# Softmax totals of the second attention with queries on partitions, and heads mixed apart and scaled while they are added

## The reference, cut to what matters

```
q, k, v = projections of the normalised x, per head
scores  = q k^T / sqrt(64), causal
pattern = softmax(scores)
z       = pattern v                       # per head, 64 wide
attn    = sum over heads of z W_O + b_O   # 128 wide
x       = x + attn * g
```

## Time and profile before

| | |
|---|---|
| median of 3 runs | 1403.93 us (1403.16 to 1404.53) |
| the profiled execution | 1399.64 us, span 1397.6 us |
| TensorE busy | 1311.2 us, 94% |
| VectorE busy | 1010.6 us, 72% |
| ScalarE, GpSimd busy | 751.9 us, 684.6 us |
| mean granted TensorE clock | 0.984 |

### The profile page before, as it was taken

One profiled execution on the slowest core, in us unless ns is written; L12 is line 12 of the kernel. 1 busy time (PEld: TensorE's weight loads), 2 busy tenths in 40 slices (PEclk: granted clock), 3 DMA queues, 4 the chain that ended last, 5 costly groups with the idle time before them and its releaser, 6 DMA issues.

```text
span 1397.6 us, 25505 instructions
## 1 busy us (share of the span) xinstructions
PE 1311.2 (94%) x9904; PEld 673.7 (48%) x9904; DVE 1010.6 (72%) x1499; ACT 751.9 (54%) x1208; POOL 684.6 (49%) x525
## 2 busy tenths in 40 slices
PE   5889999999999987989999999999999999999897
PEld 3763222222222256555555555555555555555554
DVE  7667888888888865766766766766766766766768
ACT  5476777877777873334444444344344444444343
POOL 4101150100001010568678777677677777777771
PEclk9899999999999998999999999999999999999999
DMA  1522410000000000000000000000000000000000
GB/s 36 178 100 80 125 27 1 1 1 1 1 1 1 2 1 1 1 1 1 1 1 1 1 1 1 1 1 0 1 1 1 1 1 1 1 1 1 1 16 16
DMA packets 18165, 21.50 MB, mean 15 GB/s; under 512 B 7784, under 2 KB 15872, under 8 KB 16512
## 3 DMA queue, kind: packets, MB, share of 16 engines
q1 hardware_dynamic: 18048, 19.88, 4.4%
HBM read 14.63 MB, written 5.24 MB: 14 GB/s over the span
## 4 chain that ended last, share of the span: by engine, by line
PE 43%; DVE 11%; ACT 3%; issue 1%; POOL 1%; DVEq 0%; POOLq 0%; ACTq 0%
PE psum L1839 13%; PE psum L1817 12%; DVE part_max L1981 4%; PE psum L1760 4%; DVE inv L2002 4%; PE psum L1820 3%; ACT prob L1924 3%; PE psum L1798 2%; PE psum L1747 2%; PE psum L1786 2%; PE psum L1738 1%; DVE z L2005 1%; PE psum L1740 1%; PE psum L1739 1%; PE psum L1765 1%
## 5 line engine op out<-in xcount | busy, mean ns | idle before, releaser
L1727 POOL TENSOR_TENSOR acc<-acc,prob 128x1024 f32<-128x1024 f32 (+3 forms) x250 | 493.6, 1974 | 87.9 <-ACT prob L1924 57.2
L1924 ACT ACTIVATE prob<-psum 128x1024 f32<-128x1024 f32 (+1 forms) x320 | 283.4, 897 | 350.1 <-PE psum L1820 343.6
L1981 DVE TENSOR_REDUCE part_max<-psum 128x2 f32<-128x1024 f32 (+2 forms) x320 | 337.0, 1064 | 167.9 <-PE psum L1760 83.2
L679 DVE TENSOR_SCALAR w<-psum 128x512 f32<-128x512 f32 x472 | 304.8, 687 | 59.3 <-PE psum L536 44.8
L630 ACT ACTIVATE w<-psum 128x512 f32<-128x512 f32 x552 | 293.8, 601 | 86.0 <-PE psum L536 85.7
L556 PE MATMUL psum<-w,v_cols 128*32 128x512 f32 x2048 | 274.1, 608 | 0.0
L1839 PE MATMUL psum<-prob,v_pair 128*64 128x512 f32 (+3 forms) x1280 | 250.2, 532 | 0.7 <-POOL prob L1695 0.7
L1817 PE MATMUL psum<-q_hi,k_hi 64*128 64x512 f32 (+3 forms) x640 | 138.6, 429 | 30.1 <-DVE part_max L1981 20.4
L1839 PEld LDWEIGHTS psum<-prob,v_pair 128*64 128x64 f32 x1280 | 87.4, 137 | 145.3 <-issue 134.3
L1760 PE MATMUL psum<-k_hi,q_hi 64*128 64x512 f32 (+3 forms) x640 | 132.2, 410 | 5.4 <-DVE part_max L1981 3.8
L1817 PE MATMUL psum<-q_lo,k_hi 64*128 64x512 f32 (+3 forms) x640 | 118.6, 366 | 0.0
(11 more groups left out here) (304 smaller groups left out, 1400.2 us busy)
## 6 DMA issues: line engine op xcount, KB each, us to landing
q_rows<-q_dram SPq DMA_DIRECT2D x12, 256.0 KB
k_rows<-k_dram SPq DMA_DIRECT2D x3, 1024.0 KB
x<-in_L_attn_x SPq DMA_DIRECT2D x4, 256.0 KB, 4.0
mask<-in_L_ffn_attention_mask SPq DMA_DIRECT2D x1, 1024.0 KB, 6.9
q_dram<-x_high SPq DMA_DIRECT2D x1, 1024.0 KB, 6.7
q_dram<-x_low SPq DMA_DIRECT2D x1, 1024.0 KB, 6.0
k_dram<-q_rows SPq DMA_DIRECT2D x1, 1024.0 KB, 8.1
k_dram<-k_rows SPq DMA_DIRECT2D x1, 1024.0 KB, 6.2
```

The costliest lines, as they stand in the source:

```text
L679: nc.vector.tensor_scalar(w[:, s % WR, 2 * m + 1, :], pair_bank[n % RING][1], 0.0, None, ALU.max)\
L1727: nc.gpsimd.tensor_tensor(sums, sums, prob[:, s % PR, :, q0:C], ALU.add).then_inc(summed, 1)
L1924: nc.scalar.activation(prob[:, s % PR, :, q0:C], unit_both[n % RING][:, :, q0:C], ACT.Exp, scale=SCALE)\
L1981: nc.vector.tensor_reduce(part_max[:, :, i, c], unit_both[n % RING][:, :, 0:cols], AX_X, ALU.max)\
```

## The change

The total turns round: acc is now the weight operand, 128 queries at a time, and one column of ones moves, so that side_bank gets the sums with queries on partitions, eight columns (four tiles, two heads). VectorE takes the reciprocal of 128x8 values. z is not scaled any more. The mix multiplies each head's 64 rows apart, into the two banks of its unit, and the addition to attn becomes eight fused operations that multiply a 128x128 block by its query's reciprocal and add it to attn. A mix stays one unit for a chunk; only the last chunk is mixed and finished in two units of two tiles, on the same path as the others.

```diff
-        LAST = [("mix", NP - 1, NC - 1)]
         HALVES = 2
+        LAST = [("mix", NP - 1, (NC - 1, half)) for half in range(HALVES)]
...
+        def tiles_of(g, half):
+
+            return range(half * TH, (half + 1) * TH) if g == FINAL else range(TC)
...
-        inv = sb("inv", [P, C])
+        inv = sb("inv", [P, 2, 2 * TC])
...
-                for m in range(2):
-                    last = nc.tensor.matmul(side_bank[HALF[m], :], sh.ones[:, 0:W], acc[:, g % 2, m, :],
-                                            start=True, stop=True)
+                for j in range(TC):
+                    for m in range(2):
+                        last = nc.tensor.matmul(side_bank[:, 2 * j + m:2 * j + m + 1], acc[:, g % 2, m, j * P:(j + 1) * P],
+                                                sh.ones[:, 0:1], start=True, stop=True)
                 last.then_inc(totalled, 1)
...
-            def mix(hp, qc):
-                to = room_for(("mix", hp, qc))
+            def mix(hp, qc, half):
+                to = room_for(("mix", hp, (qc, half)))
                 g = hp * NC + qc
-                if g != FINAL:
-                    pe.wait_ge(scaled, g + 1)
-                for j in range(TC):
-                    if g == FINAL and j % TH == 0:
-                        pe.wait_ge(final_scaled, j // TH + 1)
-                    last = nc.tensor.matmul(to[:, j // TH if g == FINAL else 0, j * P:(j + 1) * P],
-                                            z[:, g % 2, j * P:(j + 1) * P], wo[:, hp, :], start=True, stop=True)
-                    if g == FINAL and j % TH == TH - 1:
-                        last.then_inc(final_mixed, 1)
-                if g != FINAL:
-                    last.then_inc(unit_filled, 1)
+                pe.wait_ge(z_copied, g + 1)
+                for j in tiles_of(g, half):
+                    for m in range(2):
+                        last = nc.tensor.matmul(to[:, m, j * P:(j + 1) * P], z[HALF[m], g % 2, j * P:(j + 1) * P],
+                                                wo[HALF[m], hp, :], start=True, stop=True)
+                last.then_inc(unit_filled, 1)
...
-            def scale(g):
+            def invert(g):
                 dve.wait_ge(totalled, g + 1)
-                nc.vector.reciprocal(inv[:, :], side_bank).then_inc(inv_done, 1)
-                dve.wait_ge(inv_done, g + 1)
-                dve.wait_ge(z_copied, g + 1)
-                nc.vector.tensor_tensor(z[:, g % 2, :], z[:, g % 2, :], inv[:, :], ALU.mult).then_inc(scaled, 1)
+                nc.vector.reciprocal(inv[:, g % 2, :], side_bank[:, 0:2 * TC]).then_inc(inv_done, 1)
...
-            def add_mixed(hp, qc):
-                n = AT["mix", hp, qc]
-                tiles = slice(qc * TC, (qc + 1) * TC)
+            def add_mixed(hp, qc, half):
+                unit = ("mix", hp, (qc, half))
+                n = AT[unit]
+                g = hp * NC + qc
                 dve.wait_ge(unit_filled, n + 1)
-                nc.vector.tensor_tensor(attn[:, tiles, :], unit_both[n % RING][:, 0, :].rearrange("p (t d) -> p t d", d=D),
-                                        attn[:, tiles, :], ALU.add).then_inc(unit_freed[n % RING], 1)
-                if hp == NP - 1:
-
-                    wait_freed(dve, ("mix", hp, qc))
-                    finish(qc)
+                dve.wait_ge(inv_done, g + 1)
+                for m in range(2):
+                    for j in tiles_of(g, half):
+                        tile = attn[:, qc * TC + j, :]
+                        last = nc.vector.scalar_tensor_tensor(out=tile, in0=unit_both[n % RING][:, m, j * P:(j + 1) * P],
+                                                              scalar=inv[:, g % 2, 2 * j + m:2 * j + m + 1], in1=tile,
+                                                              op0=ALU.mult, op1=ALU.add)
+                    if m == 0:
+                        link(last)
+                last.then_inc(unit_freed[n % RING], 1)
...
-                if k == GROUPS - 1:
-                    base_final()
...
-            scale_final(0)
-            scale_final(1)
-            finish_final(0)
-            finish_final(1)
+            invert(FINAL)
+            for unit in LAST:
+                take(unit)
```

More of the change, by code:

```diff
@@ L1557, in attention1 @@
                     [("value", 0, 2)],
-                    [("project", 0, 3), ("turn", 0, 2), ("mix", 0, 0)],
+                    [("project", 0, 3), ("turn", 0, 2), ("mix", 0, (0, 0))],
                     [("value", 0, 3), ("project", 1, 0)]]
         WHOLE = [[("value", 0, 2)],
-                 [("value", 0, 3), ("mix", -1, 3)],
-                 [("mix", 0, 0), ("turn", 0, 2)],
+                 [("value", 0, 3), ("mix", -1, (3, 0))],
+                 [("mix", 0, (0, 0)), ("turn", 0, 2)],
                  [("project", 1, 0)],
                  [("project", 1, 1)],
-                 [("turn", 0, 3), ("mix", 0, 1)],
+                 [("turn", 0, 3), ("mix", 0, (1, 0))],
                  [("project", 1, 2), ("value", 1, 0)],
-                 [("mix", 0, 2), ("turn", 1, 0)],
+                 [("mix", 0, (2, 0)), ("turn", 1, 0)],
                  [("value", 1, 1)],
@@ L1633, in attention1 @@
         final_summed = sem("final_summed")
-        final_scaled = sem("final_scaled")
-        final_mixed = sem("final_mixed")
         z_copied = sem("z_copied")
@@ L1638, in attention1 @@
         inv_done = sem("inv_done1")
-        scaled = sem("scaled")
         result_step = sem("result_step")
@@ L1855, in fill @@
                 else:
-                    mix(hp, what)
+                    mix(hp, what[0], what[1])
             pe.wait_ge(sh.second_loaded, SECOND)
@@ L1929, in copy_out @@
                 if g >= 2:
-                    act.wait_ge(unit_filled, AT["mix", (g - 2) // NC, (g - 2) % NC] + 1)
+                    act.wait_ge(unit_filled, AT["mix", (g - 2) // NC, ((g - 2) % NC, 0)] + 1)
                 nc.scalar.copy(z[:, g % 2, :], out_bank).then_inc(z_copied, 1)
@@ L1955, in _, with finish @@
             link = Chain(dve, result_step)
-            def finish(qc):
-                at = slice(qc * TC, (qc + 1) * TC)
+            def finish(at):
                 link(nc.vector.tensor_tensor(attn[:, at, :], attn[:, at, :], sh.g[:, at, :], ALU.mult))
@@ L2024, in add_final @@
                     nc.vector.tensor_tensor(sums, sums, prob[:, s % PR, :, q0:C], ALU.add).then_inc(final_summed, 1)
[L2026 to L2048, removed]
@@ L2050, in add_mixed @@
-            def add_mixed(hp, qc):
-                n = AT["mix", hp, qc]
-                tiles = slice(qc * TC, (qc + 1) * TC)
-                dve.wait_ge(unit_filled, n + 1)
-                nc.vector.tensor_tensor(attn[:, tiles, :], unit_both[n % RING][:, 0, :].rearrange("p (t d) -> p t d", d=D),
-                                        attn[:, tiles, :], ALU.add).then_inc(unit_freed[n % RING], 1)
-                if hp == NP - 1:
-                    wait_freed(dve, ("mix", hp, qc))
-                    finish(qc)
+            def add_mixed(hp, qc, half):
+                unit = ("mix", hp, (qc, half))
+                n = AT[unit]
+                g = hp * NC + qc
+                dve.wait_ge(unit_filled, n + 1)
+                dve.wait_ge(inv_done, g + 1)
[8 more added lines that the diff above has]
+                last.then_inc(unit_freed[n % RING], 1)
+                if g == FINAL:
+                    wait_freed(dve, unit)
+                    finish(slice(qc * TC + half * TH, qc * TC + (half + 1) * TH))
+                elif hp == NP - 1:
+                    wait_freed(dve, unit)
+                    finish(slice(qc * TC, (qc + 1) * TC))
@@ L2069, in take @@
                 elif kind == "mix":
-                    add_mixed(hp, what)
+                    add_mixed(hp, what[0], what[1])
             dve.wait_ge(bias_done, 1)
@@ L2087, in _ @@
                 if k - 1 in ENDS:
-                    scale(ENDS.index(k - 1))
-                if k == GROUPS - 1:
-                    base_final()
+                    invert(ENDS.index(k - 1))
                 for s in range(k * PER, (k + 1) * PER):
```

## The result

The changed kernel takes 1414.82 us (median of four runs, 1412.81 to 1417.15), the kernel before, run beside it, 1403.55 us (1400.36 to 1404.53). The ratio is 1.0085 with a 95% interval of 1.0062 to 1.0107: slower, by 0.6 to 1.1%. The profiled executions, 1414.94 and 1399.64 us, lie 15.3 us apart, as do their spans (1412.9 and 1397.6).

The account below looks back on a forecast made before the run. TensorE, busy 94%, was taken as the bound, with VectorE's work worth only TensorE's waits. Terms 26.4 + 2.4 - 18.5 - 3.4 + 1.5 - 1.3 = +7.1 us gave a profiled 1406.7, median 1411 us; range 1395 to 1429.

Parts of the forecast that it names:

- Totals, +26.4: TensorE's 31 totals: sixteen float32 weight loads at 0.111 us set the pace, 0.85 us more each, +26.4 us.
- Mixing, pairs free, switches +2.4: TensorE's mix: float32 products on row halves pair at no cost; 24 added array switches of about 0.1 us, +2.4 us.
- Stalls, −18.5: TensorE's 15 stalls of scores behind VectorE's reciprocal, 23.0 us in all, shrink to 0.3 us each: −18.5 us.
- Half clock, −3.4: Two half-clock stretches of 3.4 us on TensorE, each just after a long stall, vanish with the stalls: −3.4 us.
- the three signs that I had named for a wrong forecast: Float32 loads not pacing the total, stalls returning behind the fused operations, or half-clock stretches appearing after totals.
- the 15% rival, "the clock falls at the totals": One-column totals count as rest; one in six dropping TensorE's clock adds 8.5 us, giving 1420; every third, 1429; chance 15%.
- The addition hidden, finish +1.5: VectorE's longer addition hides behind weighing, except at the last pair's finish, where the max_rows wait grows: +1.5 us.
- Tail, −1.3: From last total to last VectorE result: smaller reciprocals, mixing beside them, finishing moved; 7.7 us shrinks, −1.3 us.

Follow-up runs that it names:

- old_total: The changed kernel with the total of before (two products of 512 columns), division left wrong; 1382.58 us, ratio 0.9862 to the kernel before.
- head_by_head: The changed kernel with the mix's two loops exchanged, all tiles of one head and then the other; 1440.37 us, ratio 1.0263 to the kernel before.
- old_total_large_recip: old_total with the reciprocal again of all 128x512 values, division still wrong; 1393.01 us, ratio 0.9948 to the kernel before.
- wide_ones: The changed kernel with each product of a total moving 64 columns of ones instead of one; 1410.68 us, ratio 1.0061 to the kernel before.
- one_pass: wide_ones with the accumulated exponentials kept in one-pass float32, so each product is one load; 1380.46 us, ratio 0.9851 to the kernel before.
- double_wide: wide_ones with each total made twice, 64 moving columns; 1469.2 us, ratio 1.0483 to the kernel before.
- double_one: The changed kernel with each total made twice, one moving column; 1536.01 us, ratio 1.096 to the kernel before.
- half_adds: The changed kernel without the second head's four fused operations in each addition; 1408.84 us in a single execution.

## Why the prediction came out right, point by point

The direction, the range and the mechanism held: totals paced by float32 weight loads cost more than the stalls give back. The sum was +7.1 against +15.3 between the profiled executions, and 1411 against 1414.82 us in the medians, which lie 11.3 apart. The median came nearer than the sum in part by luck: the kernel before had been profiled in an execution 4 us below its median, the changed kernel in one at its median.

- **Totals, +26.4.** Right: 27.2. old_total against the changed kernel gives 25.6 in whole units, and the weighing behind each total begins 0.05 us more slowly, 1.6 in all. One moving column or 64 make no difference. The Trainium skill (TensorE: Matmul & The Clock Gate, Back-to-back issue gap) gives some 25 ns for 1 to 64 moving columns as the gap of isolated products, and says that in a stream of loads and products both set the spacing, which the prediction left out. At 0.111 us a load this trace bears out the second for float32; that the same page (Weight-path perf modes) keeps the fast load from float32 goes with it.
- **Mixing, pairs free, switches +2.4.** Right in kind. Pairing is shown by head_by_head and by the unchanged 37.0 us. The mix's share in old_total is 4.0, so the switches were set 1.6 too low.
- **Stalls, −18.5.** Right in size: −17.6. The cause as I gave it was too narrow. I ascribed the stalls to the reciprocal alone. It costs only 2.4 us when it is put back behind the long total and 8.5 behind the short one, and more than half of the relief comes from the rest of the change (old_total_large_recip). With the small reciprocal the length of the total makes no difference to these stalls (1.8 us of waits in the changed kernel, 1.6 in old_total), so the 26.4 us bought none of the 17.6; a longer total gives VectorE room only where the reciprocal is long.
- **Half clock, −3.4.** The step that failed. The old stretches did go with the stalls, but three new ones came behind the totals, +1.7 in place of −3.4: 5.1 of the 8.2 us by which the sum was short of the profiled pair. Half-clock stretches after the totals were also one of the three signs that I had named for a wrong forecast. I had this as the 15% rival, "the clock falls at the totals", with its mechanism right and one total in six dropping it. It was one in ten. Against it I held that no rest of 1.6 us or less had dropped the clock, nor the single one of 2.8 us. A total holds TensorE for 1.9, so the first had not decided it, and the second was chance: behind the same wait, 3.0 us long, the clock stays up in the changed kernel and in wide_ones and falls in old_total, one_pass and double_wide. wide_ones, double_one and double_wide show the cause of the new stretches, the few moving columns; which of the 31 totals it strikes is not the same in two executions (1010.0 in one, 1102.1 in the other) and stays open. The 5.1 us belong to the profiled pair: the mean granted clock of 31 further executions of the kernel before runs from 0.979 to 0.988 (1406 to 1398 us), with a median of 0.983, which is that of the changed kernel too. So in the medians the clock changes little, where the prediction had it give 3.4 back.
- **The addition hidden, finish +1.5.** The hiding is right in the main (half_adds). The finish was mis-sized: the wait for max_rows grew by 0.2 us, and the step cost 0.25. The longer addition did take its 1.5 us more, but it moved the multiplication with g past an operation of GpSimd. The changed kernel's timeline of VectorE in the last pair:

```profile
1336.68 2.29 DVE L2028 SCALAR_TENSOR_TENSOR xa<-psum,inv,xa 128x128 f32<-128x128 f32 x8 [1.28 <-PE psum L1798]
1339.00 0.69 DVE L1956 TENSOR_TENSOR xa<-xa,g 128x512 f32<-128x512 f32 x1
1339.73 2.17 DVE L1957 TENSOR_TENSOR xa<-xa,x 128x512 f32<-128x512 f32 x1
```

  The multiplication takes 0.69 us, where it took 1.92 before. Before, it began 1.37 us ahead of the end of a GpSimd addition and ended 0.55 behind that end; here it begins 0.08 us behind it. half_adds bears this out. There VectorE's four additions less bring the multiplication back beside that GpSimd operation (1332.59, 2.37 us), and it is slow again:

```profile
1333.88 1.63 DVE L1956 TENSOR_TENSOR xa<-xa,g 128x512 f32<-128x512 f32 x1
```

  It ends 0.55 us behind the end of that operation, as before, and the wait for max_rows is the 2.8 us of before. So the step that I had left out is that the longer addition is paid back by a faster multiplication. How GpSimd holds VectorE up, no run tells.
- **Tail, −1.3.** Mis-sized: −0.6. Here is the first half of the last chunk on the changed kernel's VectorE, and its last operation:

```profile
1405.61 0.21 DVE L1998 RECIPROCAL inv<-psum 128x8 f32<-128x8 f32 x1 [2.04 <-PE psum L1788]
1406.39 1.25 DVE L2028 SCALAR_TENSOR_TENSOR xa<-psum,inv,xa 128x128 f32<-128x128 f32 x4 [0.58 <-PE psum L1798]
...
1410.23 0.43 DVE L1957 TENSOR_TENSOR xa<-xa,x 128x256 f32<-128x256 f32 x1
```

  The reciprocal is small as foreseen, but after it VectorE waits another 0.58 us for the mix, which I had put beside it.
- **Ahead of the first weighing, +0.5.** Not in the sum. It lies between −2.7 and +0.9 in the kernels of the experiments, with no edit to TensorE's work there, and I give it no cause.

The terms add up: 7.1, and 5.1 clock, 0.8 whole units (29.6 against 28.8), 1.6 weighing behind totals, 0.9 stalls, −1.25 finish, 0.7 tail, 0.5 beginning make 15.4 us.

## What to carry to other kernels

Price a product by its weight loads when few columns move: a form with one moving column is free only in columns, and in float32 each product is two loads of 0.11 us; look first whether the operand can be kept in a one-pass form, which here, with 64 moving columns, turned a loss of 0.85% into a gain of 1.5%. Where a queue of TensorE products has few moving columns, try more, as far as the load covers them: here 64 cost 1.6 us in the whole units and kept the clock up behind the totals. Work taken from an engine beside the bound is worth only the stalls that it causes. Part by part that worth isn't fixed (the same reciprocal cost 2.4 us of stalls beside a long total and 8.5 us beside a short one), so test it together with the rest of the change.

## What the runs showed of the hardware that I had not expected

- A TensorE that is busy throughout can lose its clock. At totals of 32 one-column passes the granted clock fell to half in 27 of 31 places, with 64 columns moved in nearly the same time in none; at 16 passes it fell in three, with 64 columns in none.
- The same rest does not always bring it down: behind one wait of 3.0 us the clock stayed up in two kernels and fell to half in three.
- Two float32 products on different row halves share a slot of 0.111 us when they alternate in the queue (37.0 us for 512 passes), and partly even when they don't (54.6 us).
- A reciprocal of 128x512 takes 3.35 us and one of 128x8 0.20 us, so the 504 further columns cost 6.2 ns each. A multiplication or addition of 128x512 in the same program takes 0.69 us, 1.3 ns a column with its fixed part.
